# Attention features as 32x64-tile products of one batch and head, from compact transposed probabilities

## The reference

```python
# x: (128, 32, 256); a GRU over the 32 steps gives the attention's input, (128, 32, 256)
h, d = 64, 4                                   # four heads of 64 features
q, k, v = x @ Wq + bq, x @ Wk + bk, x @ Wv + bv
q, k, v = (t.reshape(B, S, d, h).transpose(0, 2, 1, 3) for t in (q, k, v))
scores = einsum('bdsh,bdth->bdst', q, k) / 2   # 32 x 32 for each batch and head
weights = softmax(scores, axis=-1)
feats = einsum('bdst,bdth->bdsh', weights, v)  # the part that the change is about
out = x + feats.reshape(B, S, F) @ Wo + bo
# behind it: 32 steps of a Runge-Kutta scan, each followed by a quantised feed-forward layer
```

## Time and profile before

| | us |
|---|---|
| median of three runs (603.88 to 604.67) | 604.24 |
| the profiled execution's own time | 603.75 |
| its span, first to last instruction | 601.7 |
| GRU stage | 0 to 209.0 |
| attention | 209.0 to 296.6 |
| second scan and feed-forward | 296.6 to 601.7 |

### The profile page before, as it was taken

The page is one execution under the profiler, slowest core; times in us unless marked ns, Lnnn a source line. Parts: engine busy times, 40 slices in busy tenths (PEclk is TensorE's granted clock), DMA queues, the critical chain, the costliest instruction groups (busy, mean ns, idle before and its releaser), DMA issues.

```text
span 601.7 us, 15742 instructions
## 1 busy us (share of the span) xinstructions
PE 572.9 (95%) x5692; PEld 521.0 (87%) x5692; DVE 513.5 (85%) x1547; ACT 390.1 (65%) x959; POOL 254.0 (42%) x401
## 2 busy tenths in 40 slices
PE   9999999999999988999978999999999999999997
PEld 8999999999999887888867788888888888888885
DVE  3777767776777768998999999999999999999996
ACT  3554454444544453464556888898898888888885
POOL 0423323233232264240155556556555555555550
PEclk9999999999999998999999999999999999999999
DMA  8500000000000000500000000000000000000001
GB/s 259 187 2 2 1 1 2 1 1 2 1 1 1 19 3 2 190 4 3 1 1 1 11 19 16 15 19 10 18 20 10 19 20 10 19 19 11 17 19 37
DMA packets 12523, 14.97 MB, mean 25 GB/s; under 512 B 1632, under 2 KB 10144, under 8 KB 12448
## 3 DMA queue, kind: packets, MB, share of 16 engines
q1 hardware_dynamic: 12448, 13.97, 7.0%
HBM read 9.78 MB, written 4.19 MB: 23 GB/s over the span
## 4 chain that ended last, share of the span: by engine, by line
PE 73%; DVE 13%; ACT 11%; issue 3%; DVEq 0%; POOL 0%; ACTq 0%; POOLq 0%
PE PS L461 23%; PE PS L313 17%; PE PS L336 13%; ACT q_s L775 5%; PE PS L436 4%; PE PS L513 4%; PE PS L534 3%; PE PS L497 3%; ACT k_s L756 2%; DVE big L955 2%; PE PS L396 2%; PE PS L319 2%; DVE PS L1072 1%; ACT PS L759 1%; DVE h_s L1161 1%
## 5 line engine op out<-in xcount | busy, mean ns | idle before, releaser
L461 PE MATMUL PS<-k_s,h_s 128*128 128x128 f32 x1024 | 160.6, 284 | 4.2 <-DVE PS L1046 2.0
L461 PEld LDWEIGHTS PS<-k_s,h_s 128*128 128x128 f32 x1024 | 131.7, 191 | 21.1 <-DVE PS L1060 9.8
L313 PE MATMUL PS<-part 128*128 128x256 f32 x900 | 115.6, 286 | 0.0
L313 PEld LDWEIGHTS PS<-part 128*128 128x128 f32 x900 | 109.8, 191 | 0.0
L756 ACT ACTIVATE k_s<-h_s 128x128 f32<-128x128 f32 x256 | 69.1, 306 | 49.8 <-DVE h_s L1161 29.0
L336 PE MATMUL PS<-big,wrk 128*128 128x128 f32 x744 | 88.4, 275 | 1.7 <-DVE big L913 1.7
L336 PEld LDWEIGHTS PS<-big,wrk 128*128 128x128 f32 x744 | 85.8, 192 | 2.3 <-DVE big L913 2.3
L1229 POOL COPY h_s<-big 128x256 f32<-128x256 f32 x32 | 21.5, 671 | 128.9 <-DVE big L913 128.9
L461 PE MATMUL PS<-h_s 128*128 128x128 f32 x384 | 74.3, 275 | 0.0
L461 PEld LDWEIGHTS PS<-h_s 128*128 128x128 f32 x384 | 58.3, 192 | 0.0
L650 ACT ACTIVATE big<-big 128x256 f32<-128x256 f32 x32 | 13.3, 416 | 63.2 <-DVE big L895 63.2
(11 more groups left out here) (189 smaller groups left out, 1244.9 us busy)
## 6 DMA issues: line engine op xcount, KB each, us to landing
out<-q_s SPq DMA_DIRECT2D x32, 128.0 KB, 1.7
x_s<-in_xT SPq DMA_DIRECT2D x14, 256.0 KB, 6.1
k_s<-in_wgT SPq DMA_DIRECT2D x1, 832.0 KB, 5.3
k_s<-in_wuT SPq DMA_DIRECT2D x1, 832.0 KB, 7.2
k_s<-in_wih SPq DMA_DIRECT2D x3, 256.0 KB, 4.1
wrk<-in_whh SPq DMA_DIRECT2D x3, 256.0 KB, 4.3
h_s<-in_wdT SPq DMA_DIRECT2D x1, 768.0 KB, 7.5
x_s<-in_xT SPq DMA_DIRECT2D x4, 128.0 KB, 3.6
```

What stands on the lines that cost most here:

```text
L313: r = pe.matmul(p, y, x, start=i == 0, stop=i == len(passes) - 1)
L461: return pe.matmul(PS[:, m, 0:128], w, x, start=False, stop=True, skip_group_check=True)
```

## The change

The features become 64 products a block, one for each batch and head: the stationary operand is 32 rows of values by 64 features, the moving operand the 32x32 transposed weights of that batch and head. Batch `j` of a group lies on its own 32 partitions and writes to a bank of its own, so the features fill half of each of four banks (4 to 7). For block 7 they lie in banks 1 and 2, two batches to a bank, and the products run in two halves with a wait between them. `PT` holds the transposed weights without the zeros, 512 columns instead of 2048; one transpose makes it, and GpSimd no longer clears it. The features lie in SBUF by batch within the group first, and the projection reads its moving operand in runs of 32 columns. VectorE's `keep_feats` waits for both of ScalarE's pieces. Values move to bank 2, projections and the weights' sums to bank 3 (some of the last projections to 0, 5, 6 and 7), and the first values no longer wait for a copied score operand.

```diff
-        PT = [big[:, 2048 + 2048 * r:4096 + 2048 * r].rearrange("p (u n) -> p u n", u=16) for r in range(2)]
+        PT = [big[:, 2048 + 512 * r:2560 + 512 * r] for r in range(2)]
...
-        feats = [PS[:, 5:7, :]] * 7 + [PS[:, 3:5, :]]
+        fb = lambda a, n: PS[:, a:a + n, :].rearrange("p b (h n) -> p (b h) n", h=2)
+        feats = [PS[:, 4:8, 0:256]] * 7 + [fb(1, 2)]
+        of_g = lambda a: a.rearrange("p (j g t) -> p g j t", j=4, g=4)
...
-        out_bank = lambda i, m: {(5, 1): 2, (6, 1): 0, (7, 0): 1, (7, 1): 2}.get((i, m), 7)
+        out_bank = lambda i, m: {(5, 1): 0, (6, 1): 5, (7, 0): 6, (7, 1): 7}.get((i, m), 3)
...
                 if (i, hf) == (0, 0):
                     pe.wait_ge(s_wv, 2)
                     pe.wait_ge(s_vs0, 1)
-                    pe.wait_ge(s_qka, 1)
...
-                for g in range(4):
-                    for hd in range(4):
-                        a = 64 * (hd % 2)
-                        r = pe.matmul(feats[i][a:a + 64, hd // 2, g * 128:(g + 1) * 128], Vs[i % 2][:, g, hd * 64:(hd + 1) * 64],
-                                      PT[i % 2][:, unit(g, hd), :], start=True, stop=True)
+                for js in ((0, 2), (1, 3)) if i == 7 else ((0, 1, 2, 3),):
+                    if js == (1, 3):
+                        r.then_inc(s_pv7, 1)
+                        pe.wait_ge(s_pv7, 1)
+                    for g in range(4):
+                        for kk in range(2):
+                            for j in js:
+                                for a in (0, 64):
+                                    hd = 2 * kk + a // 64
+                                    r = pe.matmul(feats[i][a:a + 64, j, (4 * kk + g) * T:(4 * kk + g + 1) * T],
+                                                  Vs[i % 2][quads[j], g, hd * 64:(hd + 1) * 64],
+                                                  PT[i % 2][quads[j], unit(g, hd) * T:(unit(g, hd) + 1) * T],
+                                                  start=True, stop=True)
                 r.then_inc(s_pv, 1)
...
-                    passes = [(w[:, k, ms], x[:, k, :]) for w, x in ((wo_lo, f_hi[i]), (wo_hi, f_lo[i]), (wo_hi, f_hi[i]))]
+                    passes = [(w[:, k, ms], of_g(x[:, k, :])) for w, x in ((wo_lo, f_hi[i]), (wo_hi, f_lo[i]), (wo_hi, f_hi[i]))]
...
-                if i < 2:
-                    ve.wait_ge(s_zero, i + 1)
-                else:
+                if i >= 2:
                     ve.wait_ge(s_pv, i - 1)
                 ve.wait_ge(s_P, i + 1)
-                for r in quads:
-                    o = ve.transpose(PT[i % 2][r, :, r], Pn[r, :, :])
-                o.then_inc(s_PT, 1)
+                ve.transpose(PT[i % 2], Pn.rearrange("p u n -> p (u n)")).then_inc(s_PT, 1)
...
             def keep_feats(i):
+                by_j = lambda a: a.rearrange("p (j n) -> p j n", j=4)
+                ve.wait_ge(s_fhi, 2 * i + 2)
                 for kk in range(2):
-                    ve.wait_ge(s_fhi, 2 * i + kk + 1)
-                    ve.scalar_tensor_tensor(raw(f_lo[i][:, kk, :]), feats[i][:, kk, :], ba[:, 2, kk:kk + 1],
-                                            f_hi[i][:, kk, :], ALU.add, ALU.subtract).then_inc(s_F, 1)
+                    ve.scalar_tensor_tensor(by_j(raw(f_lo[i][:, kk, :])), feats[i][:, :, kk * 128:(kk + 1) * 128],
+                                            ba[:, 2, kk:kk + 1], by_j(f_hi[i][:, kk, :]), ALU.add,
+                                            ALU.subtract).then_inc(s_F, 1)
...
-            for r in range(2):
-                po_.memset(PT[r][:, :, :], 0.0).then_inc(s_zero, 1)
```

## The result

The changed kernel takes 619.33 us (median of four runs, 616.08 to 624.23), beside 604.06 for the kernel before on the same chip (602.14 to 604.67): ratio 1.0268, interval 1.0236 to 1.0300. The forecast was 606.9 with a range of 600 to 612.5: the sign held, the size did not. The runs of the changed kernel lie 8 us apart, those of the kernel before 2.5.

What follows compares the result with a forecast made beforehand. TensorE's order of work bounds the blocks, instruction packets being a second limit. Head -3.4, four runs +5.2, run at 35 -0.1, old stall -0.5, loads +1.5: +2.7 on 603.75, 606.45; median 0.49 above: 606.9, range 600 to 612.5.

Steps and rivals of the forecast that it cites:

- Packets of 256, one ahead, over 3 us each: TensorE's instructions come in 256-entry packets, 3.2 us each; dense features and scores stall 2.0, four runs plus 1.3 each.
- The clock: Rival: each of four stalls brings half clock on TensorE, 1.6 us each, up to 613; chance 0.18.
- a clock of 0.50 after a stall: Listed sign that the forecast is wrong: TensorE at the lower clock level behind a wait for instructions.
- 1.65: At the head, the projection and the values after it take 1.65 us less at full clock, part of -3.4.
- Contention with the loads: Run at position 116, block 2: its packet shares DMA engines with weight loads; 0 to 3.6 us more, 1.5 taken.
- Features as quick as scores: Each block's 128 feature matmuls take 1.22 us like the scores, not 1.90: minus 0.68 of TensorE work.
- The head: Up to block 1's features: first projection starts at 228.85, not 230.63, at full clock; minus 3.4 us in all.
- The last block at nothing: Products in two halves cost about 0.6 more, hidden behind VectorE's chain: nothing taken, 0.6 without that cover.
- its list of positions: First packet boundaries: 12 entries into the first features, then 192, 116, 35, 210, 129 and 48 into the following ones.
- Hidden fetches: Rival: instruction packets arrive without TensorE waiting, so only work counts: -9.4, 594.8 us; chance 0.12.
- slow small products: Rival: a feature matmul costs twice the scores' 9.5 ns, so features take 2.44 us; 611.5 us, chance 0.07.
- never more than one packet between: Argument against hidden fetches: the profile's three stalls at packet ends had at most one packet between them.

Runs made afterwards that it cites:

- the kernel before with features in the middle: Kernel before, with the features of block i-1 moved between the first projection and the second half of the values: 615.78 us, ratio 1.0201.
- with the loads in halves the changed kernel: Changed kernel, with the first two feed-forward weights loaded in halves, each half a block after the one before, and later loads moved back: 620.29 us, ratio 1.0244.
- the last two kernels: Changed kernel with features moved between the values' halves and halved loads, plus 20 unneeded instructions (605.99 us), or 40 and wide warming products (606.51 us).
- the kernel with features in the middle: Changed kernel, with the features of block i-1 moved between the first projection and the second half of the values: 606.07 us, ratio 1.0038.

## Why the prediction came out as it did

*Packets of 256, one ahead, over 3 us each.* Right. Gaps stood inside the scores of blocks 1, 4 and 5 (1.89, 2.09, 1.69 us, forecast 2.0), hardly in block 3, each ended some 2.4 us after a burst, with 52 packets (forecast 53), and moved as computed when instructions were added ahead of them.

*The clock.* The step that failed: the sum has the stalls of 2.0 us with no half clock behind them. That stood among the rivals at 0.18, priced up to 613, with the reason "2.0 is shorter than the one seen" (the measured 619.33 lies above even that price), and "a clock of 0.50 after a stall" is on the text's own list of signs of being wrong. The trace has 0.50 behind gaps of 1.89, 4.50, 1.69 and even 1.30 us, and none behind 2.09 and 1.53: 16.6 us in all, TensorE busy in 16.0 of them, so about 8.0 us lost by an estimate, where the sum has nothing. Against the kernel before it is less, about 6.7 us by the mean clocks of 0.986 and 0.997 over some 610 us, because that kernel has a spell of its own, which the sum takes off with 1.65. The half clock carries the +3.50 between the runs and the +1.68 of the last projections, and most of the spread of the runs: they go from 616.08 at 0.989 to 624.23 at 0.975. That it follows idle time and not the shape of the products is supported by the kernel before with features in the middle, where waits for VectorE brought it, and by the blocks of small products without a gap, which keep the full clock. What decides between a gap that brings it and one that doesn't stays open, and the length alone does not: with the loads in halves the changed kernel has gaps of 1.90 us in blocks 1 and 2, the first with the full clock behind it (values in 1.70 us), the second with the half clock (2.93). Even one program does not fix it: beside the last two kernels the kernel before ran 22 times, nine at a mean clock of 1.000 (602.21 to 603.02 us) and thirteen at 0.997 (603.52 to 604.74), so the 1.65 that the sum takes off is paid in some executions only. One gap seen was taken as the bound for gaps that lower the clock; a single event bounds nothing.

*Contention with the loads.* Sized 1.5 of 0 to 3.6; measured 2.6, as the halved loads show. Block 2 lost 4.34 us, forecast 2.8.

*Features as quick as scores.* 1.42 us, not 1.22, so 11 ns a recorded matmul against 9.5. By the Trainium skill (TensorEngine Tiling (Array Packing), "Instruction Overhead") a matmul costs some 60 cycles, by an estimate 25 ns at 2.4 GHz; with eight tiles in use the trace has less than half of that for each. In a run that waits for a packet the 0.2 us are mostly inside the wait.

*The head.* Right to half a microsecond: -2.92 against -3.4, the projection at 230.01 where 229.6 would be the forecast put on this trace's start, no half clock there.

*The last block at nothing.* Wrong by 1.51 us: the 256 instructions of its features and the 256 of block 6 are a dense run like the others, a packet ends in it (1.30 us, 52 instructions into the features of block 7), and the half clock behind it covers their rest and the last projections. The text looked for cover in VectorE's chain and did not apply its own rule there, though its list of positions ends with this one, at 48.

*What is accounted for.* Forecast 2.7, the clock 8.0 (all of it, since the 2.7 has no half clock left), contention 1.1 beyond the forecast, 1.3 outside the stage (up to the attention, and the rest): 13.1 of the 13.9 us. The other 0.8 are not taken apart; the gap of 1.30 in the last block and the 0.5 of the head are among them.

*Rivals.* Hidden fetches and slow small products are both out, by the rows above. One reading there is loose: "never more than one packet between" the stalls holds for the first two, while the third is eight packets behind the second, as the text itself counts. The Trainium skill (Runtime: NRT & Kernel Launch, "Instruction fetch mechanics") calls the crossing of a block mostly hidden; here 14.2 us of it were not.

## What to carry to other kernels

Count instructions as well as cycles: 32 matmuls of 59 ns made 128 of 11 save array time, but 256 instructions of that kind in a row pass faster than the next 256 arrive, and the array stands for the difference. Lay runs of short instructions between long ones (here that gave back 13 of 15 us, though nothing beyond the kernel before), see that large loads do not stand in front of the fetches, and price a gap with the lower clock behind it, not by its own length. What a change frees on an idle engine is worth something only in an order that uses it: the single transpose bought the better order, which the kernel before could not have.

## What the runs showed of the hardware

- Four packets in a row let TensorE go on at 218.39, 222.03, 226.04 and 229.87 at the head of the kernel with features in the middle, 3.6 to 4.0 us apart, while the DMA engines were busy for 1% of the time: no two late packets in a row came closer there.
- A 32x32 block transpose of 128x512 takes 0.705 us, one of 32x512 took 0.701: four times the partitions at the same time.
- 82 recorded matmuls of 32x32 took 2.78 us on a single tile, 34 ns each, where the eight-tile features take 11.
- While loads of 0.8 MB were under way, the gap of block 2 was 2.6 us longer (4.50 us) than with these loads in halves, half a block apart (1.90).
- The lower clock is not a property of the program alone: the same kernel ran at a mean clock of 1.000 in nine executions and at 0.997 in thirteen, some 1.7 us apart.
